# Dense attention stages of a four-layer graph network: two buffers for each hand-over, ones written by GpSimd, chunks written out

## What is computed

```python
# end of the GIN layer
x = x / jnp.maximum(norm, 1e-12)          # then two layer norms with x + ..., the sum over edges between them
# an attention layer, three times (relu after the first two)
h = (x @ W.T).reshape(N, H, C)            # H = C = 8
alpha_s = jnp.einsum('nhc,hc->nh', h, a_src)
alpha_d = jnp.einsum('nhc,hc->nh', h, a_dst)
... e_exp over the edges ...
denom = jax.ops.segment_sum(e_exp, dst, num_segments=N)
out = jax.ops.segment_sum((e_exp / denom[dst])[:, :, None] * h[src], dst, num_segments=N)
return out.reshape(N, H * C) + b
```

## Times and profile before

| what | us |
|---|---|
| three runs | 18645.62, 18647.27, 18665.66 |
| their median | 18647.27 |
| the profiled execution, time | 18665.07 |
| its span | 18663.2 |
| PE busy in the span | 10676.6 (57%) |
| DVE busy | 8114.6 (43%) |
| GpSimd (POOL) busy | 7995.5 (43%) |
| ScalarE (ACT) busy | 4588.9 (25%) |

### The profile page before, as it was taken

One profiled execution on the slowest core, in us unless ns is written; L12 is line 12 of the kernel. 1 busy time (PEld: TensorE's weight loads), 2 busy tenths in 40 slices (PEclk: granted clock), 3 DMA queues, 4 the chain that ended last, 5 costly groups with the idle time before them and its releaser, 6 DMA issues. The chain is left out here.

```text
span 18663.2 us, 306198 instructions
## 1 busy us (share of the span) xinstructions
PE 10676.6 (57%) x80887; PEld 9284.4 (50%) x80888; DVE 8114.6 (43%) x22966; ACT 4588.9 (25%) x9661; POOL 7995.5 (43%) x8266
## 2 busy tenths in 40 slices
PE   4766677777777776878444444444444453444444
PEld 4655666665665665767333333433333343333333
DVE  4544544454444442000444444544444454444445
ACT  2333333332111110000222222222222222222222
POOL 4333333333333333433255555445545534545452
PEclk8666666777777777989555555555555555555555
DMA  3433343343443344656122222222222222222221
GB/s 110 123 119 120 121 122 120 121 122 88 110 110 102 107 108 125 210 169 212 42 65 65 65 65 65 59 53 64 63 63 63 63 52 60 64 63 64 63 63 45
DMA packets 1402619, 1721.04 MB, mean 92 GB/s; under 512 B 392504, under 2 KB 1132979, under 8 KB 1400986
## 3 DMA queue, kind: packets, MB, share of 16 engines
q1 hardware_dynamic: 753754, 705.87, 12.5%
q10 hardware_dynamic: 384064, 707.19, 11.7%
q0 software_dynamic: 263424, 292.78, 8.5%
HBM read 1347.67 MB, written 357.22 MB: 91 GB/s over the span
## 5 line engine op out<-in xcount | busy, mean ns | idle before, releaser
L2091 POOL DMA_INDIRECT rows<-gat_table,wgt x2457 | 2357.5, 960 | 2786.8 <-DVE msg L2286 1424.2
L2123 PE MATMUL bank<-ident,scratch 8*128 8x8 f32 x1386 | 389.1, 352 | 5147.2 <-DVE scratch L2230 4050.5
L2091 POOL DMA_INDIRECT Y<-gat_table,wgt x2394 | 2289.2, 956 | 2196.6 <-DVE msg L2286 1514.3
L2123 PEld LDWEIGHTS bank<-ident,scratch 8*128 8x128 f32 x1386 | 343.7, 306 | 5247.9 <-issue 5247.9
L912 POOL DMA_INDIRECT bins<-scratch,slots x1288 | 1288.4, 1000 | 2383.8 <-DVE slots L1178 1128.1
L979 PE MATMUL bank<-xT 112*64 112x120 f32 (+1 forms) x12688 | 2020.1, 330 | 301.6 <-issue 299.7
L979 PEld LDWEIGHTS bank<-xT 112*64 112x64 f32 (+1 forms) x12688 | 1865.5, 180 | 415.9 <-issue 400.8
L924 POOL DMA_INDIRECT rows<-node_table,idx x1106 | 1083.4, 980 | 1709.0 <-DMA idx<-in_src 1395.0
L1106 DVE TENSOR_TENSOR xT<-scores,xT 112x256 f32<-112x256 f32 x1256 | 528.8, 421 | 2658.2 <-remote 1747.4
L1268 ACT ACTIVATE xT<-xT 112x256 f32<-112x256 f32 x1586 | 658.1, 415 | 3934.4 <-DVE xT L1106 2611.1
L2150 PE MATMUL bank<-sel,msg 128*72 128x32 f32 x9702 | 1308.6, 309 | 0.0
(11 more groups left out here) (260 smaller groups left out, 21522.7 us busy)
## 6 DMA issues: line engine op xcount, KB each, us to landing
work<-in_dst_rows SPq DMA_DIRECT2D x693, 448.0 KB
xT<-bins ACTq DMA_DIRECT2D x1586, 119.0 KB
adj<-work ACTq DMA_DIRECT2D x598, 240.0 KB
work<-adj ACTq DMA_DIRECT2D x184, 780.0 KB
xT<-adj ACTq DMA_DIRECT2D x184, 780.0 KB
work<-near_table SPq DMA_DIRECT2D x988, 128.0 KB
near_table<-work SPq DMA_DIRECT2D x598, 128.0 KB
bins<-zeros ACTq DMA_DIRECT2D x46, 1547.0 KB, 7.8
```

The source lines that it names most:

```text
L2091: nc.gpsimd.indirect_dma_start(rows[s][:, j, :], None, gat_table, bass.IndirectOffsetOnAxis(edge_sources[:, s * G + j:s * G + j + 1], 0)). ...
L2123: nc.tensor.matmul(small[:, 64:64 + H], spread_out[:, 0, :], ident[0:H, 0:H], start=True, stop=True)
```

## The change

Second buffers are laid into `work`, which the dense stages don't use otherwise, and into `hbuf`: `means`, `xbufs`, `gbufs`, `tbufs`. PSUM banks come in pairs: `score_of` (4, 5), `row_of` (7, 6), `denominator` (0, 2), `nodes_of` (1, 3). The writer of chunk c now waits for the reader of chunk c-2. The stores have a semaphore for each buffer (`s_gtab`). L1787 goes; in `gin_dense1` GpSimd writes ones to all of `accT[D:ROW, :]` at the start, in the middle stages one chunk's at a time, after the denominator's matmul has read it. The loops of `gat_dense` are written out, and the `s_passed` increments of these stages go (one stays in `gin_dense1`). `mean` now ends with a wait for its own product. PE's order becomes denominators(c+2), forward(c) from the first chunk on; it was denominators(c), forward(c-1), which is the same after the start. ScalarE does activate(c+1) ahead of attend_act(c) or root(c+1). Reciprocals stay as they are.

```diff
+        means = [abuf[0:D, :], work[0:D, 0:CH]]
+        xbufs = [xbuf, hbuf]
+        gbufs = [gbuf, work[:, CH:CH + TC * ROW].rearrange("p (t d) -> p t d", d=ROW)]
+        tbufs = [tbuf, work[:, 2 * CH:2 * CH + TC * D].rearrange("p (t d) -> p t d", d=D)]
...
+        score_of, row_of = [bank[4], bank[5]], [bank[7], bank[6]]
         def attend_pe(pe, k, c):
             pe.wait_ge(q["x_ready"].handle, q["x_ready"].at(c + 1))
-            if due(c):
-                pe.wait_ge(q["gtile_ready"].handle, q["gtile_ready"].at(c))
-                pe.wait_ge(q["kept"].handle, q["kept"].at(c))
-            pe.sem_inc(s_passed.handle, 1)
-            nc.tensor.matmul(bank[4][0:D + 40, :], attend[k][:], xbuf[:], start=True, stop=True)
-            to_nodes(bank[7], xbuf, attend[k][:, 0:ROW], ROW).then_inc(q["scored"].handle, 1)
+            if due(c - 1):
+                pe.wait_ge(q["gtile_ready"].handle, q["gtile_ready"].at(c - 1))
+                pe.wait_ge(q["kept"].handle, q["kept"].at(c - 1))
+            nc.tensor.matmul(score_of[c % 2][0:D + 40, :], attend[k][:], xbufs[c % 2], start=True, stop=True)
+            to_nodes(row_of[c % 2], xbufs[c % 2], attend[k][:, 0:ROW], ROW).then_inc(q["scored"].handle, 1)
...
         def attend_ve(ve, c):
             ve.wait_ge(q["scored"].handle, q["scored"].at(c + 1))
-            if due(16 * c):
-                ve.wait_ge(s_tab.handle, s_tab.at(16 * c))
-            ve.sem_inc(s_passed.handle, 1)
-            nc.vector.tensor_copy(chunk(accT, LO, c), flat(bank[4][LO, :]))
-            nc.vector.tensor_scalar(chunk(accT, slice(D, ROW), c), flat(zeros[D:ROW, :]), 1.0, None, ALU.add)
-            nc.vector.tensor_copy(gbuf[:], by_tile(bank[7], ROW)).then_inc(q["gtile_ready"].handle, 1)
+            if due(c - 1):
+                ve.wait_ge(s_gtab[c % 2].handle, s_gtab[c % 2].at(16 * (c // 2)))
+            nc.vector.tensor_copy(chunk(accT, LO, c), flat(score_of[c % 2][LO, :]))
+            nc.vector.tensor_copy(gbufs[c % 2], by_tile(row_of[c % 2], ROW)).then_inc(q["gtile_ready"].handle, 1)
...
+                @block.gpsimd
+                def _(po):
+                    nc.gpsimd.memset(accT[D:ROW, :], 1.0).then_inc(q["cleared"].handle, 1)
...
                     def mean(c):
                         ve.wait_ge(q["prod_ready"].handle, q["prod_ready"].at(c + 1))
-                        nc.vector.reciprocal(inverse[:], bank[0][LO, :]).then_inc(q["inverted"].handle, 1)
+                        nc.vector.reciprocal(inverse[:], denominator[c % 2][LO, :]).then_inc(q["inverted"].handle, 1)
                         ve.wait_ge(q["inverted"].handle, q["inverted"].at(c + 1))
-                        if due(c):
-                            ve.wait_ge(q["x_ready"].handle, q["x_ready"].at(c))
-                        ve.sem_inc(s_passed.handle, 1)
-                        nc.vector.tensor_tensor(flat(abuf[LO, :]), flat(inverse), chunk(accT, LO, c), ALU.mult
+                        if due(c - 1):
+                            ve.wait_ge(q["x_ready"].handle, q["x_ready"].at(c - 1))
+                        nc.vector.tensor_tensor(flat(means[c % 2]), flat(inverse), chunk(accT, LO, c), ALU.mult
                                                 ).then_inc(q["mean_ready"].handle, 1)
+                        ve.wait_ge(q["mean_ready"].handle, q["mean_ready"].at(c + 1))
                     mean(0)
...
+                    for c in range(NCH):
+                        if c + 1 < NCH:
+                            mean(c + 1)
+                        attend_ve(ve, c) if nxt else finish(c)
...
                     denominators(0)
                     denominators(1)
-                    forward(0)
-                    with pe.Fori(2, NCH) as c:
-                        denominators(c)
-                        forward(c - 1)
-                    forward(NCH - 1)
+                    for c in range(NCH):
+                        if c + 2 < NCH:
+                            denominators(c + 2)
+                        forward(c)
...
+                    activate(0)
+                    for c in range(NCH):
+                        if c + 1 < NCH:
+                            activate(c + 1)
                         if nxt:
                             attend_act(ac, c)
...
+                        else:
+                            root(ac, c + 1)
+
+                if nxt:
+                    @block.gpsimd
+                    def _(po):
+                        for c in range(NCH):
+                            po.wait_ge(q["prod_ready"].handle, q["prod_ready"].at(c + 1))
+                            nc.gpsimd.memset(chunk(accT, slice(D, ROW), c), 1.0).then_inc(q["cleared"].handle, 1)
```

126 lines of the change are left out of this document (42 added, 84 removed).

## The result

The kernel after takes 18550.67 us (median of 5 runs, 18543.10 to 18581.37), the kernel before 18647.27 (5 runs, 18635.82 to 18665.66): the ratio is 0.9952, 95% interval 0.9937 to 0.9966, so 96.6 us less. The forecast was 18598.8 with a range from 18580 to 18642. The direction was right.

What follows compares the result with a forecast made beforehand. DVE was taken to bound the middle stages and gin_dense1, DVE and ScalarE in turn the last. Savings of 25.4 + 10.8 + 12.3 = 48.5 us from the median 18647.27 gave 18598.8 us, range 18580 to 18642.

Steps and rivals of the forecast that it cites:

- one table load: Last stage: written out, ScalarE's chunk-1 table load of 1.28 us goes; gain estimated at 0.9 us.
- In steady state they free PE and ScalarE, which don't bind: worth nothing there: Second buffers between a stage's ends: no gain, since PE needs about 5.9 us a chunk and DVE more.
- the sum of 12.7: Each middle stage: 11 chunks by 0.85 us less give 9.3, ramp 1.1, end 2.3.
- (a): Middle stage's ramp: denominator 1 no longer waits for reciprocal 0, so DVE's 1.23 us wait becomes about 0.1: -1.1.
- (b): Middle stage's end: last score no longer waits for the previous chunk's L1788; 8.55 us become 6.29, worth 2.3.
- (c): End of gin_dense1: L1769 starts at 9088.5 instead of 9089.68, no longer after DVE's L1788: -1.15 us.
- (d): Last stage's end: last finish no longer waits 2.34 us for the store of the one output tile: -2.3.
- (1): Rival: gaps stay long or PE's order holds DVE at 6.5 us; gain 36.6 us, time 18610.7; chance 0.13.
- (2): Rival: double buffers give nothing at the ends, ones' time becomes a wait; about 18630 to 18645 us; chance 0.10.
- (3): Rival: GpSimd's memsets hold DVE, 12 to 42 us back; 18611 to 18641 us; chance 0.06.
- (4): Rival: written-out code is fed late, 2.21 us a chunk in three stages; slower, 18685 us; chance 0.07.
- (5): Rival: untouched passes' code moves in memory, shifting 18100 us a tenth of a per cent either way; chance 0.12.

Runs made afterwards that it cites:

- e5: Kernel before with only the ones moved to GpSimd; stages (gin_dense1, two middle, last) 187.0, 102.8, 102.9, 131.9 us.
- e6: Kernel before with gat_dense's loops written out on DVE, PE, ScalarE and SP, nothing else; stages 198.7, 102.9, 102.8, 112.9 us.
- e7: Kernel before with loops written out and the passed-counter increments left out; stages 196.7, 101.1, 101.2, 110.8 us.
- e12: Kernel after with DVE's wait for its own product moved back behind the copies or finish; stages 184.6, 87.7, 87.8, 107.5 us.
- e8: Kernel before with loops written out, increments out, ones on GpSimd, but no second buffers, new orders or added wait; stages 185.0, 97.7, 97.8, 110.8 us.
- e3: Kernel before with only ScalarE's loop in gat_dense written out; last stage 119.6 us against 131.8, one table load left.
- e9: Kernel after with an increment, then a one-element exponential, between product wait and activation in the last stage, so table loads follow the wait; last stage 120.1 us.
- e10: Kernel after with ScalarE's old order (copies of chunk c before activation of c+1), two buffers kept; stages 184.7, 97.6, 97.9, 109.0 us.
- e11: Kernel after with one pair of banks for the scores instead of two, new order kept; stages 184.9, 96.6, 97.1, 109.0 us.
- e13: Kernel after with DVE's product wait late and the last stage's product on GpSimd; stages 184.8, 87.8, 87.9, 99.4 us, ratio to before 0.9942.
- e2: Kernel after, unchanged, timed again on chip 6; 13024.95 us against 13086.70 before, ratio 0.9947.
- e4: Kernel after with a one-element exponential before each later activation of the last stage, bringing back 23 table loads; last stage 109.0 us.
- e17: Kernel before with 64 idle increments each on PE, DVE, ScalarE and SP ahead of gin_dense1; passes 3036.3, 3091.7, 3069.6 us.

## Why the prediction was right or wrong

**Where the miss lies.** 48.5 us were forecast and 96.6 measured. Of the 48.1 between them 20.1 are in the four stages (last stage 10.5, each middle stage 3.1, gin_dense1 3.4) and 28 in stages that nobody changed. The stages alone would have made 18578.7, 1.3 below the range. Two steps of the prediction failed: "one table load" in the last stage, and "In steady state they free PE and ScalarE, which don't bind: worth nothing there"; the first moved the number, the second was hidden by the way the sum was made.

**What bounds each stage.** DVE in the first three, DVE and ScalarE in turn in the last, as said; that ScalarE's and PE's ring stood 0.06 us behind it in the middle stages was not seen. PE's 5.9 us came out right: it is what is left once the ring is open, and DVE's 6.04 lies just above it.

**Part 1, the ones.** 0.70 each off DVE's path was forecast: in gin_dense1 e5 gives 11.8 us for 13 of them, 0.91 each. The rest over 0.70 is in the copies: without the ones between them the second starts 1.04 us after the first (9022.77 - 9021.73) and no longer 1.93 (12154.22 - 12152.29 in the earlier trace rows), 0.89 less. The memset takes 1.15 us, 2.5 times the cast's value that was taken, but within the bounds of 0.46 to 1.6, and takes 5.64 us for the long one, just below the bound's 5.9. Both are hidden, as said: nothing waits for them. In a middle stage its worth depended on part 3: 1.9 alone (e5).

**Part 2, waits.** An increment was put at 0.11 to 0.13; e6 and e7 give 0.14 (gap 0.18 to 0.04). The gap before the product: 0.33, 0.18 written out, 0.03 at the end, forecast 0.05. The added wait was forecast at +0.14 to +0.26 a chunk; e12 gives 0.10 in a middle stage and 0.12 in the last (1.2 and 1.5 over 12 or 13 chunks), a little less. The 6.04 of a middle chunk for the 6.26 forecast is then 0.18 from the second copy (1.04 after the first, 1.22 taken) and the rest from shorter gaps; in gin_dense1 0.89 + 0.14 make the 1.03 a chunk that were forecast as 0.81.

**Part 3, two buffers.** "In steady state they free PE and ScalarE, which don't bind: worth nothing there" failed. It is true against the kernel before, whose DVE took 7.11, and false once the other parts have taken DVE to 6.2 or less: then the ring's 6.65 to 7.05 binds, and e8 shows the stage at 97.7 without part 3. That the sum of 12.7 came near is luck: the chain above it assumed a DVE with nothing else in its way, which is what part 3 makes true. The mistake was to compare PE's work alone with DVE's chunk. The trace of before has the ring in plain sight in the earlier trace rows: the last activation starts 1.49 us after the last product has ended (12224.92 against 12223.43), since the second of ScalarE's two copies (L1777, from 12223.92) stands before it. At the ends: (a) the ramp, forecast 1.1, is 1.2 (the second reciprocal follows at once, the 1.23 of the earlier trace rows are gone); (b) 8.55 to 5.99 is 2.56, forecast 2.3; (c) from the last activation's end to L1769 in gin_dense1, 1.30 became 0.05, 1.25 for the 1.15 forecast, but 0.97 of it came from part 1 (0.33 in e8, whose L1788 is earlier by the ones' time), so that part 3 is worth only 0.4 there; (d) the store's 2.34 us gone, as forecast.

**Sum of a middle stage.** 11 chunks by 7.11 - 6.04 = 1.07 are 11.8, ramp 1.2, end 2.6: 15.6 of the 15.8 measured, 12.7 forecast. gin_dense1: 14.2 measured, 10.8 forecast. Most of the 3.4 is 11 chunks by 1.03 for 0.81, 2.4 us; 13.5 of the 14.2 are these chunks, the 1.25 at the end and the last copies' 0.89.

**The last stage.** 12.3 forecast, 22.8 measured. The step that failed is "one table load". The prediction saw both loads of a chunk ("loads a table, activates, loads the other, takes the root") and took them for two tables that every later chunk needs. The row that it was read from, in chunk 1, was right, and so was the reason, that the loop's body serves every chunk. It holds for the later chunks in the same way: since one table serves the activation and the root, as e3's single load shows, written-out code needs neither of the two loads in any chunk. The groups of ScalarE show 24 loads; the prediction read one timeline row. The size: 12.2 us by e3, 11.1 by e9 where they are put back, against 0.9. The other terms of this stage were sound: 11.4 forecast, 10.6 left of the 22.8.

**The rivals.** (1), gaps staying long, didn't happen: they are 0.03. That DVE would be held at over 6.5 us is what e8, e10 and e11 do show, for want of ScalarE's new order or the second banks. (2), no gain at the ends: no. (3): the memsets hold nothing up; L1763 and L1902, the first of them beside a memset in six chunks, keep 1.22 and 3.33 us. The Trainium skill's "SBUF — State Buffer", section "Who interferes with whom", would have it so for an operation of GpSimd that reads nothing, and would have DVE's two-input operations wait for one that reads; e13 is that second case, 0.93 for 0.42 us. In the kernel after no operation of DVE with two SBUF inputs ran beside a memset, so the first case isn't tested. (4), late feed: no; ScalarE, PE's matmuls and DVE show no wait for "issue" in the chunks; the weight loads show 0.56 us in those of the middle stages, as they did before. (5), a shift of the untouched stages, came about: 28 us that no changed stage accounts for, 17.5 of them in the 9221 of the three passes, on the side that had two thirds of its chance of 0.12. That the place of the code is its cause isn't shown, and on chip 6 there was no such gain (e2). The sum had nothing for it.

**The range.** It left out the fast side, below 18580, as if only losses were unsure. The two steps that failed, loads and ring, were each judged from rows of one chunk, and the load's was chunk 1, which isn't typical.

## What to carry to other kernels

Before a second buffer is called worthless, follow the loop that the hand-overs make through all engines, with the order on each: its length, not any engine's busy time, is what stands next behind the bound. Where a loop's body holds two functions of ScalarE, count the table loads in the groups of the whole stage, and ask for each whether it stands behind what the engine waits for. A part tried alone can look small (the ones: 1.9 us of a middle stage) and be worth more with its partner: 0.89 a chunk over 11 chunks is an estimated 9.8 of the 15.8 us once the ring is open. Cost parts together with what binds next. And compare stages in the profile, not only whole times: code that nobody changed moved by tens of us here.

## What was not expected of the hardware

- A table load of 1.28 us costs nothing where it can be issued while ScalarE waits (e4: 23 loads, 109.0 us) and, with the load before the root, 9.8 to 12.2 us a stage where it stands behind the wait (e9, 120.1, less the exponential's 1.3; e3).
- An increment of a semaphore, on an engine's path behind a wait, costs 0.14 us (0.18 to 0.04).
- Memset of GpSimd: 1.15 us for 8x512 and 5.64 for 8x6656, 2.2 and 0.85 ns an element; its product of 64x512 takes 1.51 us.
- Idle instructions ahead of the passes, on other engines than GpSimd, moved one by 22 of 3092 us (e17, one execution), and the same kernels' passes take 2084 to 2091 us on one chip and 3030 to 3098 on another.
